# One core, hybrid block: the first tile's FFN and mamba front inside attention, scan tiles of 4 states x 32 channels, and small products moved to GpSimd

## The reference

```python
x = hidden_states                                  # [2, 1024, 256]
x = x + attention(layernorm(x))                    # gated delta rule, 16 heads of 128
x = x + ffn(layernorm(x))                          # silu(x Wg) * (x Wu), 1024 hidden, then Wd
x = x + mamba(layernorm(x))                        # 512 channels, 16 states
x = x + ffn(layernorm(x))                          # the same weights again

# mamba, per sequence; conv is causal with 4 taps
xc = silu(conv(un @ Wx) + cb);  z = un @ Wz        # un = layernorm(rmsnorm(x) ...) scaled
B, C, d = split(xc @ x_proj)                       # 16, 16 and 1 rows
dt = softplus(d * dt_w + dt_b);  A = -exp(A_log)
h_t = exp(dt_t * A) * h_{t-1} + (dt_t * xc_t) * B_t   # [512 channels, 16 states]
y_t = sum over states(h_t * C_t) + D * xc_t
out = (y * silu(z)) @ out_proj + residual
```

## Time and profile before

| | |
|---|---|
| timed, median of 3 | 2581.08 us |
| profiled execution | 2578.36 us, span 2576.3 us |
| PE busy | 2390.3 us (93% of the span) |
| DVE busy | 2037.5 us (79%) |
| ACT busy | 1702.4 us (66%) |
| POOL busy | 1160.5 us (45%) |
| DMA | 104.65 MB, mean 41 GB/s |

### The profile page before, as it was taken

How to read it: one execution, slowest core, us unless ns; L and a number is a source line. 1 busy time by engine, 2 the same in 40 slices (tenths; PEclk the granted TensorE clock), 3 DMA queues, 4 the chain that set the end, 5 groups by cost and what they waited for, 6 DMA issues and landing times.

```text
span 2576.3 us, 86928 instructions
## 1 busy us (share of the span) xinstructions
PE 2390.3 (93%) x38320; PEld 1411.5 (55%) x38320; DVE 2037.5 (79%) x2968; ACT 1702.4 (66%) x3416; POOL 1160.5 (45%) x925
## 2 busy tenths in 40 slices
PE   6699999999999999999999999978989899998888
PEld 2366666666666666666666666653433333333333
DVE  3778888888888887888888888841359999999981
ACT  3667888788778777887788788743465646455332
POOL 0445545554554454445545554510044646555530
PEclk8899999999999999999999999999999999999999
DMA  1000000000000000000000000010023324333320
GB/s 57 23 10 13 13 14 24 13 13 24 13 13 13 24 13 13 13 24 13 13 13 24 13 13 17 6 54 27 0 95 95 127 92 134 99 119 114 125 84 17
DMA packets 52007, 104.65 MB, mean 41 GB/s; under 512 B 7084, under 2 KB 11948, under 8 KB 51376
## 3 DMA queue, kind: packets, MB, share of 16 engines
q1 hardware_dynamic: 51632, 99.11, 11.9%
HBM read 96.72 MB, written 2.37 MB: 38 GB/s over the span
## 4 chain that ended last, share of the span: by engine, by line
PE 58%; DVE 23%; ACT 10%; issue 7%; POOL 1%; DMA 0%; SPq 0%; DVEq 0%; ACTq 0%; POOLq 0%
PE bank L382 9%; DVE hs L1751 6%; PE bank L486 5%; PE pair L609 4%; DVE cv L694 4%; PE bank L643 4%; PE bank L453 4%; PE bank L1568 4%; PE pair L597 3%; PE bank L579 2%; PE bank L422 2%; ACT Y L1070 2%; PE bank L1490 2%; DVE kq L782 2%; PE pair L1490 2%
## 5 line engine op out<-in xcount | busy, mean ns | idle before, releaser
L694 DVE SCALAR_TENSOR_TENSOR cv<-raw,taps,cv 128x1024 f32<-128x1024 f32 x288 | 396.8, 1378 | 20.3 <-ACT cv L958 18.5
L2057 POOL TENSOR_TENSOR dBu<-dtu,Bn 128x1024 f32<-128x1024 f32 x128 | 306.4, 2396 | 224.0 <-DVE hc L1758 223.9
L382 PE MATMUL bank<-xn,W 128*128 128x512 f32 x768 | 372.2, 615 | 0.0
L1955 ACT ACTIVATE bank<-dtv,m_A 128x512 f32<-128x512 f32 x256 | 174.3, 687 | 212.4 <-DVE hs L1751 211.8
L1568 PE MATMUL bank<-hc,eye 128*128 128x512 f32 x512 | 255.4, 626 | 62.3 <-DVE hc L1758 62.2
L1254 POOL TENSOR_TENSOR kq<-kq,tot 128x512 f32<-128x512 f32 x128 | 219.0, 1711 | 191.0 <-PE bank L453 191.0
L1231 POOL TENSOR_TENSOR R<-kq,gate 128x1024 f32<-128x1024 f32 x32 | 77.5, 2421 | 456.8 <-ACT gate L1024 456.8
L1568 PEld LDWEIGHTS bank<-hc,eye 128*128 128x128 f32 x512 | 93.0, 193 | 211.4 <-DVE hc L1758 123.2
L382 PEld LDWEIGHTS bank<-xn,W 128*128 128x128 f32 x768 | 135.8, 193 | 121.3 <-issue 112.8
L1758 DVE TENSOR_TENSOR hc<-hs,Cn 128x1024 f32<-128x1024 f32 x128 | 169.7, 1326 | 11.3 <-PE bank L1568 7.0
L957 ACT ACTIVATE raw<-bank 128x512 f32<-128x512 f32 x192 | 114.7, 597 | 96.1 <-PE bank L382 93.7
(11 more groups left out here) (269 smaller groups left out, 5464.7 us busy)
## 6 DMA issues: line engine op xcount, KB each, us to landing
Bn<-ssm_rows SPq DMA_DIRECT2D x128, 256.0 KB, 3.5
Cn<-ssm_rows SPq DMA_DIRECT2D x128, 256.0 KB, 3.2
W<-in_head_w SPq DMA_DIRECT2D x32, 448.0 KB, 3.6
WO<-in_out_w SPq DMA_DIRECT2D x32, 192.0 KB, 2.3
xT<-in_xT SPq DMA_DIRECT2D x1, 2048.0 KB, 7.7
out_xT<-xT SPq DMA_DIRECT2D x4, 512.0 KB, 3.7
xn<-in_w_gate SPq DMA_DIRECT2D x1, 1024.0 KB, 5.7
xn<-in_w_up SPq DMA_DIRECT2D x1, 1024.0 KB, 8.6
```

The source lines that it names most:

```text
L382: m = pe.matmul(psum[bank][:, :], w[:, (kind * KT + k) * P:(kind * KT + k + 1) * P], xn[:, k, b, cols], start=k == 0, stop=k == KT - 1)
L694: dve.scalar_tensor_tensor(cv[m % 2][:, :, :], raw[m % 2][:, :, i:i + SEG], taps[:, h, KQV[n], i:i + 1], cv[m % 2][:, :, :], MUL, ADD).the ...
L1955: act.activation(psum[A_BANKS[at % NA]][:, :], dtv[u % 2][:, j, :], ACT.Exp, scale=m_A[:, j, n:n + 1]).then_inc(dA_set.sem)
L2057: pool.tensor_tensor(dBu[at % AHEAD][:, :, :], dtu[s][:, half * DT2:(half + 1) * DT2, :], spread(Bn[at % DEEP][:, :], 1, DT2), MUL).then_i ...
```

## The change

It has six parts.

1. *The first FFN of tile 0 goes into attention's middle.* Before, its steps stood in attention's drain, behind the last units (3249 to 3459 on the scale of the table `EARLY_AT`). Its own functions (`first_tensor`, `first_vector`, `first_scalar`) work block by block in units 20 to 27, and `first_weights` loads each block's three pieces of weights. The former `EARLY_AT` row is replaced by one with 37 places.
2. *The first front (tile 0) goes into attention's end.* `front` becomes a function of its own on each engine and is called from `att_drive` with a second row of `EARLY_AT`; it uses attention's PSUM ring and memory that attention no longer needs.
3. *All large FFN weights have tiles of their own* (`wg`, `wu`, `wd`, `w_o`), loaded behind the barrier; nothing of the FFN's weights lies in attention's memory any more. The second FFN (w = 1) and all later ones run in the second part.
4. *A scan item is 4 states of 32 channels*, no longer one state of 128. The front writes dt and dtu to memory (`ssm_wide`), and SP reads them back as `dt_wide` and `dtu_wide`, where partition 32 s + c holds channel c of a group of 32, whatever the state s. B and C tiles hold 4 states, 32 partitions each, and there are only four of each in a unit. PE adds with a 128 x 32 selection matrix `sel` into a quarter of a bank.
5. *The scan writes its state back over its decay in PSUM*, and the product with C is done for each item apart, from PSUM.
6. *POOL* makes the scaling of the fronts' `mu` and the dt sums (except for tile 0) and the FFNs' `xh` (from w = 2, `FFN_DVE`).

Items run in another order: all 16 states of one 128-channel tile (16 items), then the next tile. The tables `FRONT_AT` and `FFN_AT` are new; a line of each:

```diff
 FRONT_AT = [
-    [-201.9, -182.6, -171.2, -80, -77.2, -77.2, -72.2, ...
+    [131.5541, 135.0487, 135.0487, 137.3885, 138.9477, ...
 FFN_AT = [
-    [-220, -211.6, -202.5, -194.7, -184.6, -181.6, -154.3, ...
+    [-52.4215, 64.2648, 64.2648, 64.2648, 95.7294, 101.226, ...
...
-            att_drive(ffn_tensor(pe, take, held), conv(0), ...
+            att_drive((first_tensor(pe, take, held), front_tensor(pe, take, held)(0)), conv(0), ...
...
+        def first_weights(sp, j):
+            if j:
+                sp.wait_ge(*first_down.at(j - 1, KT - 1))
...
+            sp.dma_start(fw_gate, a["w_gate"][:, :, j * P:(j + 1) * P]).then_inc(ffn_loaded.sem, 16)
+            sp.dma_start(fw_up, a["w_up"][:, :, j * P:(j + 1) * P]).then_inc(ffn_loaded.sem, 16)
+            sp.dma_start(fw_down, a["w_down"][:, j, :]).then_inc(ffn_loaded.sem, 16)
...
+        def first_tensor(pe, take, held):
...
+            for j in range(NJ):
...
+                for k in range(KT):
+                    m = pe.matmul(psum[bank][:, :], fw_gate[:, k, :], fx[:, k, :], start=k == 0, stop=k == KT - 1)
...
+                for k in range(KT):
+                    m = pe.matmul(psum[bank][:, :], fw_up[:, k, :], fx[:, k, :], start=k == 0, stop=k == KT - 1)
...
+                for k in range(KT):
+                    bank = take()
...
+                    pe.matmul(psum[bank][:, :], fw_down[:, k * P:(k + 1) * P], fh).then_inc(first_down.sem)
...
-            def gather(u, p):
-                pe.wait_ge(*hc_set.at(u * PAIRS + p))
-                for jj in range(DT2):
-                    m = pe.matmul(psum[Y_BANKS[jj]][:, :], eye[:, :], hc[(u * PAIRS + p) % BACK][:, jj, :], start=False,
-                                  stop=p % HALF_P == HALF_P - 1, skip_group_check=True)
+            def gather(n, sg):
+                group = n * SG + sg
+                pe.wait_ge(*hc_set.at(2 * group + 1, DT2 - 1))
+                for q in range(QS):
+                    m = pe.matmul(psum[Y_BANKS[n % 2]][quad(q), :], sel[:, :],
+                                  hc[(2 * group + q // DT2) % BACK][:, q % DT2, :], start=False, stop=sg == SG - 1,
+                                  skip_group_check=True)
...
-                    dve.tensor_tensor_scan(hs[p % BACK][:, jj, :], psum[A_BANKS[at % NA]][:, :], dBu[p % AHEAD][:, jj, :],
+                    h = psum[A_BANKS[at % NA]]
+                    dve.tensor_tensor_scan(h[:, :], h[:, :], dBu[p % AHEAD][:, jj, :],
                                            carry[:, b, i:i + 1] if seg else 0.0, MUL, ADD).then_inc(h_set.sem)
...
-                        dve.tensor_tensor(hc[p % BACK][:, :, :], hs[p % BACK][:, :, :], spread(Cn[p % DEEP][:, :], 1, DT2),
-                                          MUL).then_inc(hc_set.sem)
+                        for k in range(DT2):
+                            dve.wait_ge(*h_set.at(p * DT2 + k))
+                            dve.tensor_tensor(hc[p % BACK][:, k, :], psum[A_BANKS[(p * DT2 + k) % NA]][:, :],
+                                              Cn[sg][:, :], MUL).then_inc(hc_set.sem)
...
+            def carry_out(at):
+                u, i = divmod(at, ITEMS)
+                seg, b = divmod(u, NB)
+                act.wait_ge(*hc_set.at(at // DT2, at % DT2))
+                if seg == 0:
+                    act.activation(carry[:, b, i:i + 1], psum[A_BANKS[at % NA]][:, SEG - 1:SEG],
+                                   ACT.Copy).then_inc(carry_set.sem)
...
                 if at >= NA:
-                    act.wait_ge(*h_set.at(at - NA))
+                    carry_out(at - NA)
...
+        FFN_DVE = 2
...
+                if w >= FFN_DVE:
+                    pool.wait_ge(*f_inv.at(w))
+                    pool.tensor_tensor(xh[:, :, :], f_cen_t[:, :, :], spread(f_rstd[:, :], 1, KT),
+                                       MUL).then_inc(xh_later.sem)
...
+                    if u:
+                        pool.wait_ge(*dt_log.at(u, p))
+                        pool.tensor_tensor(dtv[:, :, :], dtv[:, :, :], soft[:, :, :], ADD).then_inc(dt_later.sem)
...
+                wide(0)
+                for sg in range(SG):
+                    rows(sg)
+                wide(1)
+                if u == 0:
+                    for t, name in ((wg, "w_gate"), (wu, "w_up"), (wd, "w_down")):
+                        sp.dma_start(t[:, :, :], a[name]).then_inc(ffn_loaded.sem, 16)
+                    sp.dma_start(w_o[:, :, :], a["w_o"]).then_inc(wo_m_loaded.sem, 16)
```

629 lines of the change are left out of this document (399 added, 230 removed), and 47 rows, old and new, of tables (EARLY_AT, FFN_AT, FRONT_AT).

## The result

The changed kernel takes 2563.04 us, the median of 5 runs (2559.73 to 2566.89). The ratio to the kernel before is 0.9933, with a 95% interval of [0.9915, 0.9951]. It is 18 us faster where I forecast 55. The profiled execution took 2566.89 us with a span of 2565.1, so it is 44 us longer than the 2521 that I worked out. In the first 200 us its granted clock is 0.87, before the change 0.91, in the other changed kernels between 0.86 and 0.92. Its first output sum comes at 193.0 us, before the change at 188.9, in the other changed kernels between 184.3 and 191.9. So 4 of the 44 us have nothing to do with the change.

The account below looks back on a forecast made before the run. PE was taken to bound attention, DVE the scans. Scans running as if from 1851 us, a 597 us phase and 73 us after gave a 2521 us span, 2526 beside timed runs, 55 us faster; 8-in-10 range 2490 to 2582.

Parts of the forecast that it names:

- a barrier well off 1819 us: Sign that the forecast is wrong: the barrier ahead of the scans was expected at 1819 us.
- Attention longer by 48 us: Attention: first FFN's matmuls 41.3 us, plus statistics and table loads, move unit 30's output sum from 1703.2 to 1751 us.
- the first FFN disturbs attention: Rival, chance 0.07: its chain over four engines costs 3 us above the matmuls in eight units, 24 us, 2550 us.
- The drain: Attention's end: front's convolution, last unit's state, output rescaling and second softplus follow one another, from 1751 to the barrier at 1819.
- Behind the barrier: Loads: first scan at 1831 us, weights there at 1852, fourth scan at 1856; a stall of 20, 47 us won.
- no stall: Rival, chance 0.12: 32-partition loads issue faster or land sooner, the fourth scan does not wait; 20 us less, 2506.
- Scan phase, DVE's work: Scans: scalings and dt sums off DVE, product with C from PSUM in halves, PSUM scans free; -17.9 us.
- Held banks: Scan phase on ACT: banks freed only after half products delay exponentials about 1.2 us at silu and softplus stretches; +16 us.
- The slower rival: Held banks make DVE wait in the scans: 64 us more with PSUM scans, 2590 us, phase above 656; chance 0.11.
- The gathers overlap: PE in scans: a gather's 8 matmuls in column tiles run beside each other, between 0.9 and 3.4 us; nothing counted.
- The end in 73 us: After the last product with C: chain of 22, the rest 48.4, clock 3 us; 73 us in place of 79.4.

Follow-up runs that it names:

- thin_first: Changed kernel with the 96 matmuls of the first FFN inside attention on 64 instead of 512 columns; 0.9929 of the kernel before.
- down_later: Changed kernel with the first FFN's down products inside attention placed 0.18 of a unit (some 5 us) later; 0.9929 of the kernel before.
- z_after: Changed kernel with PE's four z projections and the B, C, dt product behind and between the last state's first three chunks; 0.9962 of the kernel before.
- front_behind: Changed kernel with the whole first front, from its first projection, behind the last unit's state; 1.0010 of the kernel before.
- weights_first: Changed kernel with the four weight loads issued right behind the first wide tiles and first rows of B and C; 0.9891 of the kernel before.
- gates_later: Changed kernel with the second FFN's steps, first gate to last down product, moved from 95.7..132.1 to 112.5..133 in the orders; 0.9934 of the kernel before.
- state_sbuf: Changed kernel with each scan writing its state over its dBu tile in SBUF instead of its decay in PSUM; 1.0187 of the kernel before.
- front1_earlier: Changed kernel with the second front's last ten steps some 10 us earlier in the orders; 0.9945 of the kernel before.
- pe_busy: Changed kernel with two added zero matmuls of 512 columns behind each gather but a channel tile's last (96 in all); 1.0025 of the kernel before.

## Why the prediction was wrong

The direction was right, and the chain of steps (front ahead of state, barrier, fourth scan behind the weights, DVE at the scans) came as written. The size was off, by 55 against 18 us: terms that I had each taken near their lower end. My own sign of an error, a barrier well off 1819 us, came true: it is at 1846.5, 4 us of it from the low clock at the start.

- *Attention longer by 48 us*: the failed step. From output sum 0 to output sum 30 it is 1576.1 us against 1514.2, so 62. PE is busy for 51.6 us more: I had priced a matmul at 0.43 us from a pipelined run of groups, but these, in single groups among others, take 0.48, 46.1 us in all. PE's idle time grows by another 10 us, for which my sum had nothing, and 8.3 us of waits are for the down product alone. I even took free PE time as a possible gain of up to 8 us. The rival "the first FFN disturbs attention", to which I gave 0.07, holds for some 10 us of its 24. The step's reasoning failed too, that PE's work is added one for one: thin_first takes 29 us of it away and wins 6, down_later takes 7.6 us of the wait away and wins nothing that can be told. So the 62 us are measured and the two parts of them read from the trace; what sets them stays open.
- *The drain*: the table load, the convolution (9.12 us), the state and the output were sized from undisturbed rows. PE's projections stand between them (9.5 and 7.0 us ahead of the state, 3.6 us inside it), and I had counted DVE's side alone. The two pieces up to output sum 31 are 10.6 us longer than forecast; DVE waits 2.6 us for PE behind the convolution and 5.0 us between two chunks. That these projections make the 10.6 us is read from the timeline and not shown: z_after moved the last 7.0 us of them and the 3.6 us, and output sum 31 came 6.8 us later. Of the four places tried mine is the best: front_behind is 19.3 us later, the other two 7 to 8.
- *Behind the barrier*: issue at 0.467 us a load was right, the weights were issued 23.0 us behind the first load. But the loads ahead of them were still moving, at 213 GB/s, and the weights landed 38.3 us behind it where I had 33. And the first gate group took 3.7 us where I had 1.9, at a granted clock of 0.50 (the window from 1880 us). weights_first takes 15.8 us off the stall, and the phase is 17.4 us shorter; gates_later takes off as much and wins nothing. So the rival "no stall" priced an earlier landing about right, and would have won nothing by other users alone.
- *Scan phase, DVE's work*: -17.9 us forecast, busy time fell by 25 (569.9 to 544, the first three scans included). PSUM scans at +12 ns and halves without outliers were right. *Held banks*: +16 us forecast. Outside the first stall the waits for exponentials grew from 3.7 us before to 14.3, and freeing the banks earlier (state_sbuf) took only 2.5 of them away. So 10.6 us came where I had 16, and my reason is shown for a small part of them at most; what makes the rest stays open. The slower rival fell: the phase stayed at 628.
- *Scan phase, other waits*: not in the sum. New are the 8.7 us at the second unit, where dt and dtu come back through memory, and some 17 us for FFN and output sums; DVE's idle time is 61.7 us where my sum had 44.6 (28.6 before, 16 added). front1_earlier and pe_busy show that these waits hang together: taking one away makes the next one longer, adding to PE makes all longer.
- *The gathers overlap*: right. The 8 matmuls of one gather, in PE's timeline, end in 1.06 us, beside each other, where I had between 0.9 and 3.4:

```profile
2305.63 0.62 PE L1687 MATMUL bank<-cen,sel 128*32 128x512 f32 x2
2305.64 0.62 PE L1687 MATMUL bank<-hc,sel 128*32 128x512 f32 x2
2306.08 0.60 PE L1687 MATMUL bank<-cen,sel 128*32 128x512 f32 x2
2306.09 0.60 PE L1687 MATMUL bank<-hc,sel 128*32 128x512 f32 x2
```

- *The end in 73 us*: right, 73.8.

## What to carry to other kernels

When work moves onto an engine that is 97% busy, count its own time at the price of an isolated instance (0.48, not 0.43 us), add the waits of its chain, grant no free time, and don't expect the time back when that work is made smaller (29 us less gave 6). Behind a barrier ask two questions of a queue of loads, how fast they are issued and how fast they move; put first what many instructions wait for. In a phase in which several chains stand one behind another, one wait less is its length won only where its cause goes: here 15.8 us less stall made the phase 17.4 us shorter where the data came earlier, and no shorter where only the order of their users changed. Such a difference is read from the windows of the phase; the ratios of two kernels leave it open by 6 us either way here.

## What the runs showed of the hardware

- Loads into 32 partitions moved 213 GB/s with the DMA share at 1.08, the same bytes into 128 partitions 364, and weights 438.
- Half products and convolution steps with two SBUF inputs that began while a POOL operation had more than a quarter of a microsecond to run ended 0.55 us behind it (all but one of 58), however short they are alone (0.75 us in the row shown, 0.68 for the half products). The Trainium skill, SBUF — State Buffer, section "SBUF: two separate sides", calls this pair of ports an exclusive lock; the 77 us of state_sbuf agree. One PSUM input was enough to avoid it (675 ns, at most 683, with 234 of 256 beside a POOL operation). It cost nothing either: from two SBUF inputs the median is 680 ns.
- A scan in place in PSUM takes 1218 ns against 1206 into SBUF.
- Shortening matmuls in a full stage went with a granted clock of 0.96 instead of 1.00, and 10 of the 29 us came back as longer times of the other matmuls.
